# One block from the projections to the output: score maxima of groups 0 and 1 inside the last projection steps

## The reference

```
def reference(x, ctx, Wq, bq, Wk, bk, Wv, bv, Wo, bo, clip_x, clip_down, w_gate, w_up, w_down):
    # x, ctx: (4, 1024, 512) float32; 16 heads of 32; 256 text tokens behind 768 image tokens
    q = (layernorm(x) @ Wq + bq); k = (ctx @ Wk + bk); v = (ctx @ Wv + bv)      # 16 heads each
    scores = where(trinity_mask, q k^T / sqrt(32), -inf)     # image rows: own third of the image;
    attn = softmax(scores)                                   # text rows: all image, causal text
    x = x + (attn @ v) @ Wo + bo
    xn = layernorm(x)
    # int8-like fake quantisation of xn, of the rows of w_gate, w_up, w_down, and of h
    h = silu(xq @ gate^T) * (xq @ up^T)                      # 1408 wide
    return x + hq @ down^T
```

## Time and profile before

| what | value |
|---|---|
| median of 3 runs | 1153.02 us (1149.35 to 1153.77) |
| the profiled execution | 1152.52 us, its span 1150.7 us |
| mean granted clock of PE | 0.95 |
| busy share of the span | PE 92%, DVE 65%, POOL 56%, ACT 44% |

### The profile page before, as it was taken

How to read it: one execution, slowest core, us unless ns; L and a number is a source line. 1 busy time by engine, 2 the same in 40 slices (tenths; PEclk the granted TensorE clock), 3 DMA queues, 4 the chain that set the end, 5 groups by cost and what they waited for, 6 DMA issues and landing times. The chain is left out here.

```text
span 1150.7 us, 18228 instructions
## 1 busy us (share of the span) xinstructions
PE 1055.0 (92%) x6550; PEld 708.0 (62%) x6550; DVE 751.8 (65%) x1351; ACT 511.7 (44%) x882; POOL 639.5 (56%) x347
## 2 busy tenths in 40 slices
PE   5999999999629989999999999899985799999898
PEld 4888888888516656666666666457764344444343
DVE  5665456654319657777777777335978487777785
ACT  3322223222102657766676667661101455554553
POOL 3434454344440979999999999654754112100373
PEclk8999999999955999999999999899998799999899
DMA  5987777856699896867888773448997454100876
GB/s 203 319 257 231 224 279 256 271 170 196 208 175 191 177 225 154 188 154 174 182 180 192 166 157 110 117 129 239 308 276 182 118 200 148 36 1 1 326 240 220
DMA packets 129619, 218.08 MB, mean 190 GB/s; under 512 B 29320, under 2 KB 55688, under 8 KB 128330
## 3 DMA queue, kind: packets, MB, share of 16 engines
q1 hardware_dynamic: 129546, 217.12, 68.4%
HBM read 134.76 MB, written 77.74 MB: 185 GB/s over the span
## 5 line engine op out<-in xcount | busy, mean ns | idle before, releaser
L780 ACT ACTIVATE a_probs<-a_banks 128x512 f32<-128x512 f32 (+2 forms) x512 | 233.7, 535 | 130.9 <-PE a_banks L996 105.3
L713 POOL TENSOR_TENSOR a_pair_sums<-a_probs,a_probs 128x2048 f32<-128x2048 f32 x48 | 222.0, 4625 | 67.0 <-ACT a_probs L780 58.9
L855 DVE TENSOR_REDUCE a_max<-a_banks 128x2 f32<-128x512 f32 x192 | 123.1, 685 | 54.4 <-PE a_banks L967 54.1
L996 PE MATMUL a_banks<-a_queries,a_keys 97*128 97x512 f32 x384 | 146.7, 426 | 10.7 <-ACT a_probs L780 6.6
L967 PE MATMUL a_banks<-a_keys,a_queries 96*128 96x256 f32 x384 | 85.7, 318 | 33.1 <-DMA a_queries<-q_split 33.1
L972 PE MATMUL a_banks<-a_keys,a_queries 96*128 96x512 f32 (+1 forms) x256 | 114.9, 463 | 0.0
L851 DVE CUSTOM_DVE_ANT_0 a_masked_scores<-a_banks,kept_mask 128x384 f32<-128x384 f32 (+1 forms) x128 | 79.5, 621 | 49.4 <-PE a_banks L972 49.1
L855 DVE TENSOR_REDUCE a_max_parts<-a_banks 128x1 f32<-128x512 f32 x128 | 87.9, 687 | 24.8 <-PE a_banks L972 20.9
L967 PEld LDWEIGHTS a_banks<-a_keys,a_queries 96*128 96x128 f32 x384 | 69.9, 204 | 55.0 <-DMA a_queries<-q_split 33.8
L1369 POOL TENSOR_TENSOR d_out<-d_out,f_x 128x512 f32<-128x512 f32 x28 | 42.6, 1548 | 96.6 <-DVE d_out L1397 96.6
L225 POOL TENSOR_SCALAR p_x<-p_x,p_neg_mean,p_rstd 128x512 f32<-128x512 f32 x32 | 28.2, 895 | 121.8 <-DVE p_rstd L330 121.8
(11 more groups left out here) (173 smaller groups left out, 2207.2 us busy)
## 6 DMA issues: line engine op xcount, KB each, us to landing
a_keys<-k_split SPq DMA_DIRECT2D x48, 512.0 KB, 8.2
a_queries<-q_split SPq DMA_DIRECT2D x48, 512.0 KB, 14.3
f_x<-x_scratch SPq DMA_DIRECT2D x14, 1024.0 KB, 7.8
p_c<-in_ctx_dram SPq DMA_DIRECT2D x8, 1024.0 KB, 8.8
p_x<-in_x_dram SPq DMA_DIRECT2D x8, 1024.0 KB, 10.9
v_scratch<-p_v_stage SPq DMA_DIRECT2D x16, 512.0 KB, 9.1
k_split<-p_stage_hi SPq DMA_DIRECT2D x16, 512.0 KB, 4.2
k_split<-p_stage_lo SPq DMA_DIRECT2D x16, 512.0 KB, 5.3
```

The source lines that it names most:

```text
L713: pool.tensor_tensor(PP[u % 2], PR[2 * c % 4], PR[(2 * c + 1) % 4], ALU.add).then_inc(paired, 1)
L780: act.activation(PR[kt % 4][:, j, 0:w], STB[:, n % NST, 0:w], ACT.Exp, scale=SCALE).then_inc(edone, 1)
L855: dve.tensor_reduce(out, src, AX.X, ALU.max).then_inc(wfree, 1)
L996: op = pe.matmul(out.rearrange("p (c t) -> p c t", t=SIT), keys, q, start=True, stop=True)
```

## The change

`project` and `attend_output` are no longer blocks; each returns one function per engine, and one block runs the one behind the other on each engine, with no meeting between.

- The projections use 5 banks (0, 1, 2, 6, 7; `NB = 5`, `PB`), leaving 3, 4, 5 as work banks for pieces. There is one buffer for ctx (`CX`), one for its transpose (`CT`) and one for that of x (`XT`) instead of two each, and two staging pairs instead of four, shared by k and q. All buffers lie in the arenas of attention.
- The loop has four steps, four are written out.
- Pieces of groups 0 and 1 stand in steps 5 to 7: two behind each QUERY result of step 5; four behind each VALUE result and one behind each QUERY result of step 6; four behind each VALUE and three behind each QUERY of step 7 (8, 16, 4, 16, 12). `turn_maxima(0)` stands behind the first pieces of step 7.
- The 12 first `score_t` stand alone, behind the last piece.
- LayerNorm's statistics are made among QUERY: `moments` behind item 0, `deviations` behind item 2. POOL quantises first and norms x afterwards.
- The turn of the maxima goes from slot 1 to slot 3. Slots 0 to 2 of group 0 hold no pieces; groups 2, 3, 4 have their 28 pieces in seven slots each, four a slot, so group 0 holds 20 and groups 1 and 2 hold 32 each. From group 3 on it is as before.
- SP loads the stacks of groups 0 and 1 in steps 4 to 6, that of group 2 and the values of 0 and 1 in step 7. The ones rows (L704) are set in `project`. `shift_rows(i+1)` goes behind `store(i, 0)`.

```diff
+NB = 5
+EARLY = 4
+PB = (0, 1, 2, 6, 7)
-TURN_SLOT = 1
+TURN_SLOT = 3
+CATCH_UP, SHORT = 3, 7
...
+        FIRST = [(n, item) for n, items in ((EARLY + 1, range(KT, 2 * KT)), (EARLY + 2, range(2 * KT)), (EARLY + 3, range(2 * KT)))
+                 for item in items]
+        COUNT = (2,) * 4 + (4,) * 4 + (1,) * 4 + (4,) * 4 + (3,) * 4
...
+            slot = NKT * i + kt - TURN_SLOT
+            if 0 <= slot < CATCH_UP * SHORT:
+                g, part = 2 + slot // SHORT, slot % SHORT
+                return [(g, k) for k in range(part * NPC // SHORT, (part + 1) * NPC // SHORT)]
...
             # PE, a projection step
                 for t in range(TT):
-                    tokens_out("v", CT[u], t, claim(u, n, VALUE + t))
+                    tokens_out("v", CT, t, claim(u, n, VALUE + t))
+                    for i, k in A.early(n, t):
+                        A.scores(pe, i, k)
+                    if t == 0 and not more(n, 1):
+                        A.turn_maxima(pe, 0)
...
             # SP, the end of step 7
+                stage_store(n, 0)
+                stage_store(n, 1)
...
+                    for i in range(2):
+                        A.load_values(sp, i)
+                    for part in range(3):
+                        A.load_stack(sp, 2, part)
...
                 stage_store(n, 2)
                 stage_store(n, 3)
+                    for part in range(3, 6):
+                        A.load_stack(sp, 2, part)
...
             # SP, attention
             for i in range(NGRP):
-                if i + 1 < NGRP:
-                    shift_rows(i + 1)
                 if i == 0:
-                    load_stacks(3)
-                    load_values(3)
+                    front.ffn_last(sp)
+                    for row in range(6):
+                        load_stack(sp, 3, row)
                 store(i, 0)
+                if i + 1 < NGRP:
+                    shift_rows(sp, i + 1)
                 store(i, 1)
...
             # POOL, before the first pair of probabilities
+                if u == 0:
+                    for q in front.sout:
+                        pool.wait_ge(q, 32 * (2 * NCH + 1))
```

More of the change, by code:

```diff
@@ L166, in _, with step @@
                 sp.dma_start(BQK[:, 1, :], bk.rearrange("(m p) -> p m", p=P)).then_inc(ldb, 16)
-            sp.wait_ge(wlo, 3)
-            load_c(1, 1)
+            sp.wait_ge(free, NB + KT)
+            load_c(1)
             load_x(1, 1)
             ffn_load(0, 0, 0)
-            def step(b, u, tail, final):
+            def step(b, u):
                 n = 2 * b + u
+                late = n - EARLY if isinstance(n, int) else None
+                last = not more(n, 1)
+                if late == 0:
+                    for q in sout:
+                        sp.wait_ge(q, 32 * 5)
                 for i in range(2):
@@ L176, in step @@
                     d = vs.rearrange("(n t p) c -> n p t c", t=TT, p=P)[n][:, 2 * i:2 * i + 2, :]
[L177 to L178 removed]
+                    sp.dma_start(d, VST[i]).then_inc(vout[i], 16)
+                    if last and i == 0:
+                        A.shift_rows(sp, 0)
+                    A.load_early(sp, late, i)
+                if more(n, 2):
                     s.reach(sp, free, NB + at(n) + XTURN + KT)
[L180 removed]
@@ new lines, in step @@
+                if more(n, 2):
+                    s.reach(sp, free, NB + at(n) + CTURN + KT)
+                    load_c(n + 2)
+                if late == 2:
+                    sp.wait_ge(full, at(n) + CTURN + KT)
+                    for part in range(3):
+                        A.load_stack(sp, 1, part)
+                stage_store(n, 2)
+                A.load_early(sp, late, 3)
+                stage_store(n, 3)
+                if last:
+                    for part in range(3, 6):
+                        A.load_stack(sp, 2, part)
+                else:
+                    ffn_store(b, u)
@@ new lines, in load_early, with sync @@
+        def load_early(sp, late, place):
+            part = 4 * late + place if late is not None else 9
+            if part < 6:
+                load_stack(sp, 0, part)
+            elif part < 9:
+                load_stack(sp, 1, part - 3)
+        A.load_early = load_early
+        A.load_stack, A.load_values, A.shift_rows, A.ones_row, A.early = load_stack, load_values, shift_rows, ones_row, early
+        A.wfree, A.pieces, A.reduced, A.masked = wfree, 0, 0, 0
+        def sync(sp, front):
@@ new lines, in attend_output, with scores @@
+        A.vector = vector
+        def scores(pe, i, k):
+            n = A.pieces
+            j, m = PIECES[k]
+            if k == 0:
+                pe.wait_ge(stk[i % 4], LOADS * (i // 4 + 1))
+            pe.wait_ge(wfree, n + 1)
+            out = WB[:, n % NWK, :]
+            keys = KS[i % 4][0:QROWS, j, :]
+            queries = lambda t: QS[i % 4][0:QROWS, j, t * P:(t + 1) * P]
+            if m < 3:
+                for half in range(2):
+                    op = pe.matmul(out[:, half * SIT:(half + 1) * SIT], queries(2 * m + half),
+                                   keys[:, m * SIT:(m + 1) * SIT], start=True, stop=True)
+            else:
+                t, part = 6 + (m - 3) // 2, (m - 3) % 2
+                k0, k1 = 512 * part, min(512 * (part + 1), (t + 1) * P)
+                op = pe.matmul(out[:, 0:k1 - k0], queries(t), keys[:, k0:k1], start=True, stop=True)
+            op.then_inc(wfull, 1)
+            A.pieces += 1
@@ L1009, in values @@
                     pe.wait_ge(ifree, 3 * i + kt // 2)
+                if kt == 0 and i == 0:
+                    for bank in (6, 7):
+                        pe.wait_ge(front.free, front.cleared(bank))
                 if kt == 0:
```

629 lines of the change are left out of this document (329 added, 300 removed).

## The result

| | before | after |
|---|---|---|
| median, us | 1152.76 (8 runs) | 1158.59 (8 runs) |
| ratio to before, 95% interval | | 1.006 (1.0044 to 1.0075) |
| profiled execution, us (span) | 1152.52 (1150.7) | 1161.12 (1159.4) |

A forecast was written before the change was run, and what follows sets the result against it. PE bounds the kernel, busy to nine tenths except around 307.1 to 457.1 us. With all parts summed, group 3 starts at 426.8 instead of 457.1: 1152.5 - 30.3 = 1122.2, forecast 1122 us, range 1107 to 1134.

The forecast's parts named there:

- Part 1: Between projections and group 0: the meeting, the loads behind it and the DVE-bound maxima go, 67.2 us.
- Part 2: Steps 5 to 7: pieces of groups 0 and 1, waits and turn cost 22.6 us, between 14 and 28.
- Part 3: Projection steps: five banks, single buffers and LayerNorm among QUERY cost nothing; range 0 to 10 us, taken as 0.
- rival B: Steps 4 and 5: the queue overflows, PE loses 8 to 12 us more, 1132 us; chance 0.15.
- rival C: All eight steps: ACT waits for KEY's store before QUERY 0; 5 us a step gives 1162 us; chance 0.05.
- Part 4: Ramp behind the projections: 12 `score_t` at ACT's pace, so `values` of group 0 starts at about P + 8.3.
- P: The time at which the projections end, forecast at 329.7 us.
- Part 5: Group 0: group 1's shift row waits behind a full queue until P + 34.1; some 13 us of hole.
- rival A: Group 0: queue clear in time, POOL sets the pace, group 1 at P + 34.8; 1110.5 us; chance 0.27.
- Part 6: Groups 1 and 2: 32 pieces instead of 28, 25.3 us each, shift rows on an empty queue.
- Part 7: Steady groups: turn in slot 3 finds an empty queue; 0 to +4 us over twelve groups, taken as 0.
- the projections up to step 3 are longer than before: Steps up to 3: a sign that, if seen, would make the prediction wrong altogether; no size given.

The follow-up runs named there:

- experiment 2: Changed kernel with LayerNorm's statistics and ScalarE's root back ahead of the keys: 1143.99 us, 0.9913.
- experiment 11: Changed kernel, down rows apart, x behind keys' stores, turn in slot 1 from group 2, every stack behind its shift row, statistics among queries: 1160.46 us, 1.0059.
- Experiment 3: Kernel before, eight banks kept, with LayerNorm's statistics moved among the queries and GpSimd's norm behind its quantising: 1167.36 us, 1.0116.
- 1: Changed kernel with the quantised down rows of steps 0 to 4 written to a place of their own: 1151.9 us, 0.9993.
- Experiment 7: Changed kernel with statistics back ahead of the keys and the next x loaded behind the keys' two stores: 1141.6 us, 0.9893.
- 4: Changed kernel with the six loads of stack 3 issued behind the shift row of group 1: 1163.43 us, 1.0087.
- 5: Changed kernel with the shift rows of groups 1 and 2 issued ahead of stacks 3 and 4 respectively: 1153.93 us, 0.9996.
- experiment 12: Changed kernel: statistics ahead of keys, down rows apart, x behind keys' stores, slot 1 turn from group 2, stacks 3, 4 behind rows, stack 5 split: 1120.7 us.

## Why the prediction was wrong

- **Part 1** (67.2 us go): right. No stretch without matmuls is left there.
- **Part 2** (22.6 us of pieces, waits and the turn): right in its small terms. The fourth piece behind a result waits 0.61 to 0.90 us, nine times for the eight forecast. The piece behind `moments` was put at 2.2 us (2.4 in the sum) and came to 5.00. Most of that is ScalarE's wait for the keys' store, not `moments`: with the statistics moved away (2) 3.28 us remain, and with them there but ScalarE not waiting (11) it is 2.27, as forecast.
- **Part 3** ("nothing", range 0 to 10) **is the step that failed**. The steps took 24.9 us more than forecast (7.3, 14.7 and 2.9). The term "LayerNorm among QUERY: nothing" has 14.1 of them: with the statistics at their old place (2) the three differences fall by 5.1, 6.9 and 2.1. Five banks and the rest have some 2, and what remains in step 5 is the queue's (rival B). I asked of each part whether its operation had a free bank, and found 0.5 us in hand at QUERY 0. I never asked what LayerNorm's 4.4 us had covered on VectorE at the old place. It was the load of the weights, the end of a ring so nearly as long as the step that it was late three times in eight already before (3.3 us). Experiment 3 shows the move in the kernel before, together with GpSimd's order (+13 us, 10.1 of its trace in the projections), 2 shows it undone (-14.6), 1 shows that it acts through the ring in steps 0 to 4. The sentence "if that cover is gone a step costs 1 to 4 us" had about the price (1.9 us), but for VALUE's cover of GpSimd's norm, which holds in the changed kernel and fails only in experiment 3 (1.0 to 1.1 us a step), and not for this one.
- **Rival B** (the queue in steps 4 and 5, 0.15) had half of step 5: stores landed after up to 12.1 us, where 8.2 was the longest before, and rival C's wait of ScalarE for the keys' store came, in two steps of eight. Experiment 7 takes 4.9 us of it away by order alone, so "full but not over" was true of the sum and no help to the one store that somebody waits for.
- **Part 4**: P + 9.4 for P + 8.3.
- **Part 5**: the mechanism was right, one term mis-sized. The row's hole is 13.97 us (some 13 forecast), but it ends at P + 42.6 and not P + 34.1: the queue took 8.5 us longer. The slow stretch of 372 to 384 us costs some 6.4 where the scales' term has about 3, which is 3.4 of the 8.5 (by the estimate above); the rest was not traced to a term. PE got there later too, at P + 28.6 and not P + 21: GpSimd's first pair waited 8.2 us for the last q store, ScalarE 5.17 for GpSimd, PE 2.98 for ScalarE, with a clock of 0.50 from 365 to 375. Without a hole at its row group 0 still takes 29.6 to 34.9 us in the experiments, where rival A had 26.5; what sets that was not found. Experiments 4 and 5 add what the part did not see: the queue is short over groups 0 to 2 as a sum, so removing the hole at one row moves it to the next, unless the loads are spread (12).
- **Part 6**: right, 25.5 and 25.1.
- **Part 7** ("0 to +4, I take 0"): +5.6, beyond its range. Slot 3 has a clear queue, as forecast, and still costs 0.3 us a group, and 0.7 to 1.0 more in each fourth from `invert`. Its score items are narrower than those of slot 1 (256 columns for 512 in this trace); that the turn's item shows beside them for this reason is argued, not tried.

My statement on what would prove it wrong altogether, "the projections up to step 3 are longer than before", came true. That the six edits of experiment 12 end at 1120.7, near the forecast's 1122, is chance: the forecast had 13 us of hole in group 0; that kernel has no hole there and takes 31.8 us for the group all the same.

## What to carry to other kernels

Before moving work off a place, write down what waits behind it on the same engine there: work that ends just before a load lands is that load's cover, and moving it exposes the load. Look for rings (compute, store, wait for landing, load into the same buffer), add the terms that are work or transfer and compare with the period; where they nearly fill it (35.3 of 36.17 us here, before, with the load at the 9.5 us of the trace after), a delay inside the ring is paid each time around. With a queue near full, taking away one late transfer shows the next: spread the loads over the periods that have room, and put ahead what somebody waits for.

## What was not expected of the hardware

VectorE's 128x4 `tensor_scalar` of LayerNorm takes 0.17 us ahead of the keys (all eight in experiment 2) and 2.48 us as a median among the queries, where GpSimd is quantising. It ends with GpSimd's instruction: 128.85 + 2.48 = 131.33 against 125.93 + 5.36 = 131.29.

```profile
128.85 2.48 DVE L419 TENSOR_SCALAR p_ln<-p_mean_var 128x4 f32<-128x4 f32 x1
```
```profile
125.93 5.36 POOL L326 TENSOR_SCALAR p_gate_up_q<-p_gate_up_raw 88x2048 bf16<-88x2048 f32 x1 [0.20 <-POOL p_down_raw L323]
```

The same holds at 166.89 (169.37 against 169.35) and 251.11 (253.73 against 253.71), and for all seven of experiment 3, which take 3.94 to 3.98 us. The Trainium skill ("SBUF — State Buffer", Who interferes with whom) says that VectorE and GpSimd share a port pair as an exclusive lock, which some VectorE forms, `tensor_scalar` among them, can ask for, and that the loser blocks for the other's whole instruction; this trace agrees, to 0.04 us. By itself the longer operation cost nothing in the steps of experiment 11; how much of the ring's 2.3 us at the q store comes from it was not tried.
